# A deformable convolution sampled tile row by tile row in a loop, with part of the hat functions on GpSimd

## What is computed

```python
off1 = conv2d(x, w_off1, b_off1, stride=1, pad=1)          # 18 offsets per pixel: (dy, dx) for 9 taps
out = relu(bn_inf(deform_conv(x, off1, w_dc1, 1, 2, 2), g1, beta1, m1, v1))
off2 = conv2d(out, w_off2, b_off2, stride=1, pad=1)
out = relu(bn_inf(deform_conv(out, off2, w_dc2, 1, 2, 2), g2, beta2, m2, v2) + x)
# deform_conv: for each pixel and tap, the image is read at (y + 2*ky - 2 + dy, x + 2*kx - 2 + dx),
# bilinearly between four pixels, zero outside; then a 64 x 64 product per tap, summed over the taps
```

## Time and profile before

| | |
|---|---|
| median of 3 runs | 894.47 us (892.66 to 895.07) |
| the profiled execution | 889.64 us, span 887.6 us, mean granted TensorE clock 0.86 |
| first sampler, 40 to 255 us | 214.5 us |
| second sampler, 286 to 503 us | 216.9 us |
| attention, experts and the end, from 503 us | 384 us |
| TensorE busy, matmuls | 728.3 us, 18,746 |
| VectorE, ScalarE, GpSimd busy | 484.3, 417.0, 161.4 us |

### The profile page before, as it was taken

One profiled execution on the slowest core, in us unless ns is written; L12 is line 12 of the kernel. 1 busy time (PEld: TensorE's weight loads), 2 busy tenths in 40 slices (PEclk: granted clock), 3 DMA queues, 4 the chain that ended last, 5 costly groups with the idle time before them and its releaser, 6 DMA issues.

```text
span 887.6 us, 40461 instructions
## 1 busy us (share of the span) xinstructions
PE 728.3 (82%) x18746; PEld 567.3 (64%) x18746; DVE 484.3 (55%) x840; ACT 417.0 (47%) x830; POOL 161.4 (18%) x190
## 2 busy tenths in 40 slices
PE   6787877788767887778788656999999999999546
PEld 2355555566633455555566545999999999998433
DVE  0565554455604645446455564666666666666654
ACT  1665455554315554546544143445445445545442
POOL 7000000000030000000000153343443443341300
PEclk8889878866769798887976578999999999999669
DMA  5400000000004000000000170000000000000002
GB/s 171 82 4 5 4 4 5 5 4 4 5 6 81 4 5 4 4 4 4 5 4 4 29 193 1 1 2 1 0 0 0 0 0 0 0 0 0 0 1 96
DMA packets 7835, 16.58 MB, mean 19 GB/s; under 512 B 1982, under 2 KB 5950, under 8 KB 7286
## 3 DMA queue, kind: packets, MB, share of 16 engines
q1 hardware_dynamic: 7678, 14.21, 6.3%
HBM read 10.34 MB, written 3.87 MB: 16 GB/s over the span
## 4 chain that ended last, share of the span: by engine, by line
PE 76%; issue 10%; DVE 6%; ACT 5%; POOL 1%; DMA 1%; SPq 0%; DVEq 0%
PE banks L227 20%; PE banks L145 14%; PE banks L696 7%; PE banks L680 7%; PE banks L726 6%; PE banks L458 4%; PE banks L737 4%; PE banks L716 3%; PE banks L691 2%; PE banks L180 2%; PE banks L166 2%; PE banks L707 2%; ACT hx L273 1%; DVE norm_stats L629 1%; ACT hy L278 1%
## 5 line engine op out<-in xcount | busy, mean ns | idle before, releaser
L227 PE MATMUL banks<-s,y 32*64 32x96 f32 (+9 forms) x10752 | 191.1, 268 | 66.0 <-issue 65.9
L318 DVE TENSOR_TENSOR s<-hy,hx 128x384 f32<-128x384 f32 (+3 forms) x336 | 144.4, 476 | 183.4 <-PE banks L227 181.8
L227 PEld LDWEIGHTS banks<-s,y 32*64 32x64 f32 x10752 | 160.2, 154 | 109.9 <-issue 100.2
L145 PE MATMUL banks<-w_dc,tiled 64*32 64x192 f32 x3584 | 130.2, 412 | 20.3 <-issue 13.7
L268 ACT COPY y<-banks 128x384 f32<-128x384 f32 x192 | 81.8, 484 | 114.0 <-PE banks L145 114.0
L145 PEld LDWEIGHTS banks<-w_dc,tiled 64*32 64x32 f32 x3584 | 74.3, 131 | 53.8 <-issue 26.6
L794 ACT COPY hy<-banks 128x512 f32<-128x512 f32 x64 | 37.6, 588 | 116.7 <-PE banks L726 116.7
L278 ACT ACTIVATE hy<-banks 128x512 f32<-128x512 f32 (+2 forms) x144 | 72.9, 583 | 38.4 <-PE banks L180 38.3
L898 POOL TENSOR_TENSOR y<-y,stats 128x1024 f32<-128x1024 f32 x33 | 62.8, 1902 | 142.2 <-DVE stats L839 142.2
L273 ACT ACTIVATE hx<-banks 128x384 f32<-128x384 f32 x144 | 61.4, 505 | 31.8 <-PE banks L166 23.9
L680 PE MATMUL banks<-src,s 128*128 (+1 forms) x560 | 75.0, 279 | 1.1 <-ACT src L617 1.1
(11 more groups left out here) (137 smaller groups left out, 876.9 us busy)
## 6 DMA issues: line engine op xcount, KB each, us to landing
src<-in_x_dram SPq DMA_DIRECT2D x4, 578.0 KB, 5.5
y<-in_w_dram SPq DMA_DIRECT2D x1, 2080.0 KB
off<-in_w_dram SPq DMA_DIRECT2D x2, 1024.0 KB
out_dram<-tokens SPq DMA_DIRECT2D x4, 512.0 KB, 2.6
offsets_dram<-tokens SPq DMA_DIRECT2D x32, 54.0 KB
off<-offsets_dram SPq DMA_DIRECT2D x16, 108.0 KB
w_dc<-in_w_dc_dram SPq DMA_DIRECT2D x2, 288.0 KB, 6.0
y<-in_w_attn_dram SPq DMA_DIRECT2D x1, 512.0 KB, 4.9
```

The source lines that it names most:

```text
L145: last = nc.tensor.matmul(m.ps[32 * j:32 * j + 32, FIRST_BANK + (count + g) % RING, (col % 2) * 192:(col % 2) * 192 + 192], m.tiled[rows, ...
L227: last = nc.tensor.matmul(out[:, r0:r0 + strip.n, first:first + width], m.y[32 * j:32 * j + 32, g, (s // 3) % 2 * Y_SLOTS + strip.slot, co ...
L318: nc.vector.tensor_tensor(dst, hy, hx[:, :, r0:r0 + strip.n, :], ALU.mult).then_inc(cv.s_ready, 1)
```

## The change

The sampler's order becomes tile row, then tap: 72 steps per convolution, and a step's window is not cut at the half. TensorE runs the eight tile rows as a hardware loop; the other engines stay unrolled.

- The output of one tile row covers 12 rows. ScalarE copies four of them per tile row (eight in the first) from PSUM into `tokens`, VectorE adds the eight that overlap, ScalarE or VectorE finish four rows of the image, and TensorE clears 4 banks again. `prime`, `copied` and `added` order this.
- Columns: only the four new rows of a window are computed (`hx_near` keeps the other four from the tile row before, two slots of nine taps); new constant matrices `near_sel` (1 MB, a DMA more) and more rows of `places` make them with 4 matmuls for all four tiles. `off` is cleared by VectorE first, and SyncE waits for that before the loads of convolution 1.
- One item (x, y or weighted) now fills two banks at once and is taken by one ScalarE instruction; there are two such pairs. `s` and `hy` have three slots.
- GpSimd makes the hats in x (`sampler_pool`, 78 per convolution), copies one tile row at a time into `stage`, and doesn't tile the whole image any more.
- TensorE waits for both halves of the offsets before the sampler.
- `all_*`, the way for large offsets, is kept and not run here.

```diff
+AHEAD = 2
+STEP_WEIGHTED = {0: (2, 1, 0), 4: (0, 0, 1), 5: (0, 1, 1), 6: (1, 0, 1), 7: (1, 1, 1), 8: (2, 0, 1)}
+def slot_banks(m, k):
+    return m.ps[:, FIRST_BANK + 2 * (k % 2):FIRST_BANK + 2 * (k % 2) + 2, :]
...
+    with pe.Fori(0, TR) as i:
+        k = BEFORE_LOOP
+        for t in range(TAPS):
+            later, tap = divmod(t + AHEAD, TAPS)
+            pe.wait_ge(cv.emptied, i * PER_ROW + (k - 1))
+            columns_near(nc, m, cv, k, tap, new_rows(cv, tap) + TILE_ROWS * later, TILE_ROWS, i)
+            k += 1
+            pe.wait_ge(cv.emptied, i * PER_ROW + (k - 1))
+            rows_near(nc, m, cv, k, tap, first_row(cv, tap) + TILE_ROWS * later, i)
+            k += 1
+            if t == 0:
+                pe.wait_ge(cv.copied, i + COPIED_FROM)
+                pe.wait_ge(cv.added, i + (ADDED_FROM - 1))
+                pe.wait_ge(cv.cleared, 1)
+                for bank in range(PAIRS):
+                    nc.tensor.matmul(m.ps[:, bank, 0:OUT_ROWS * W], m.zeros[:, 0:P], m.zeros[:, 0:OUT_ROWS * W],
+                                     start=True, stop=True, skip_group_check=True)
+            if t in STEP_WEIGHTED:
+
+                pe.wait_ge(cv.emptied, i * PER_ROW + (k - 1))
...
+            pe.wait_ge(cv.s_ready, i * (2 * TAPS) + (2 * t + 2))
+            for col in range(TC):
+                first, width, skip = near_columns(cv, col, kx)
+                for j in range(4):
+                    for g in range(2):
...
+            last.then_inc(cv.sampled, 1)
+            if t in STEP_WEIGHTED:
+                weighted_near(nc, m, cv, k, *STEP_WEIGHTED[t][0:2])
+                k += 1
...
+                if t == TAPS - 1 and kind == "w" and tile_row < TR - 1:
+                    act.wait_ge(cv.sampled, TAPS * (tile_row + 1))
+                    first, n = (TILE_ROWS, 2 * TILE_ROWS) if tile_row == 0 else (2 * TILE_ROWS, TILE_ROWS)
+                    at = TILE_ROWS * (tile_row - 1) + first
+                    nc.scalar.copy(sum_rows(m, at, n), out_rows(m, first, n)).then_inc(cv.copied, 1)
+                item_act(nc, act, m, cv, k)
...
+    for n in range(TR * TAPS):
+        if n + 1 < TR * TAPS:
+            hats(n + 1)
+        if n % TAPS == 0 and n // TAPS >= 2:
+            below = n // TAPS - 1
+            dve.wait_ge(cv.sampled, n)
+            dve.wait_ge(cv.copied, COPIED_FROM + below + 1)
+            first = TILE_ROWS * (below - 1)
+            nc.vector.tensor_tensor(sum_rows(m, first, 2 * TILE_ROWS), sum_rows(m, first, 2 * TILE_ROWS),
+                                    out_rows(m, 0, 2 * TILE_ROWS), ALU.add).then_inc(cv.added, 1)
+            cv.rows_dve(dve, below - 1)
+        weights(n)
...
+def sampler_pool(nc, pool, m, cv):
+    old = 2 * cv.reach
+    for tap, tile_row in X_HATS:
+        pool.wait_ge(cv.emptied, EMPTIED_AT["x", tap, tile_row])
+        x = x_block(m, cv, tap, tile_row) if tile_row >= 0 else x_block(m, cv, tap, -1, TILE_ROWS - old, old)
+        nc.gpsimd.tensor_scalar(x, x, 1.0, 1.0, ALU.min, ALU.subtract).then_inc(cv.x_hats, 1)
+        if tap == 3 and tile_row >= 0:
+            pool.wait_ge(cv.filled, EMPTIED_AT["w", 2, 1, tile_row])
+            stage_pool(nc, m, cv, min(tile_row + 1, TR - 1))
```

More of the change, by code:

```diff
@@ L55, in near_strips @@
[L55 to L71, removed]
@@ L74, in near_columns @@
[L74 to L125, removed]
@@ new lines, in step_items @@
+def step_items(tile_row, tap):
+    items = coords(TAPS * tile_row + tap + AHEAD)
+    if tap in STEP_WEIGHTED:
+        ky, part, later = STEP_WEIGHTED[tap]
+        items.append(("w", ky, part, tile_row + later))
+    return items
+BEFORE_LOOP = len(FIRST_WEIGHTED) + len(FIRST_COORDS)
+PER_ROW = sum(len(step_items(0, tap)) for tap in range(TAPS))
+ITEMS = FIRST_WEIGHTED + FIRST_COORDS + [
+    item for tile_row in range(TR) for tap in range(TAPS) for item in step_items(tile_row, tap)]
+EMPTIED_AT = {item: k + 1 for k, item in enumerate(ITEMS)}
@@ new lines, in columns_all @@
+def columns_all(nc, pe, m, cv, count, h, tap, col):
+    pe.wait_ge(cv.all_emptied, count - RING + 2)
+    for g in range(2):
+        rows = group_rows(g, 1)
+        nc.tensor.matmul(m.ps[:, FIRST_BANK + (count + g) % RING, :],
+                         m.sel[rows, (TILE_COLS * col - 2 * (tap % 3) + 4) // 2, :],
+                         m.off[rows, tap, HALF_ROWS * W * h:HALF_ROWS * W * (h + 1)],
+                         start=True, stop=True, skip_group_check=True).then_inc(cv.all_filled, 1)
@@ new lines, in rows_all @@
+def rows_all(nc, pe, m, cv, count, h, tap, tile_row):
+    pe.wait_ge(cv.all_emptied, count - RING + 2)
+    for g in range(2):
+        rows = group_rows(g, 0)
+        nc.tensor.matmul(m.ps[:, FIRST_BANK + (count + g) % RING, :],
+                         m.sel[rows, (TILE_ROWS * tile_row - 2 * (tap // 3) + 4) // 2, :],
+                         m.off[rows, tap, HALF_ROWS * W * h:HALF_ROWS * W * (h + 1)],
+                         start=True, stop=True, skip_group_check=True).then_inc(cv.all_filled, 1)
@@ L334 @@
-ALL_SLOTS = 2
-class Row:
-    def __init__(self, tile_row, h):
-        self.tile_row, self.first, self.n, self.at = tile_row, HALF_ROWS * h, HALF_ROWS, 0
 def all_pe(nc, pe, m, cv):
-    count, n = FIRST_ITEMS, 0
+    count, n = 0, 0
     pe.wait_ge(cv.tiled, TILED)
-    pe.wait_ge(cv.moved[1], MOVES)
+    pe.wait_ge(cv.emptied, len(FIRST_WEIGHTED))
+    for half in range(HALVES):
+        pe.wait_ge(cv.moved[half], MOVES)
     for h in range(HALVES):
```

577 lines of the change are left out of this document (349 added, 228 removed).

## The result

The changed kernel takes 981.06 us (median of 4 runs, 977.49 to 985.23) where the kernel before took 894.77 (4 runs beside it): ratio 1.095, interval 1.089 to 1.102. The forecast was 933, slower by 4.3%. The direction was right; the loss is twice as large.

What follows compares the result with a forecast made beforehand. TensorE was taken as the bound, fed with code in the samplers. Looped, a serial chain would set rows of 28.0 us: first sampler +14.5, second +21, end +2, so +38 us and 933; range 878 to 998.

Steps and rivals of the forecast that it cites:

- If the body stays in place as the attention body does: TensorE's sampler loops: about 1,730 instructions stay held, so the code feed of 3.74 us per page falls away; called likelier.
- R1: Sampler loop body does not stay and code is fetched again: 992 us, or 952 with every page fetched; chance 0.25.
- The chain of 3.11 us per weighted step: Taps 5 to 8: samples, weighted fill, weighted eviction, column eviction run serially, 3.11 us a step at the upper clock level.
- The whole row: One sampler tile row: 25.9 us at the upper clock level, 31.8 at the lower, 28.0 at clock 0.80.
- The ten items ahead of the first row, 4.2 us: Start of each sampler: ten coordinate items at ScalarE's pitch of 0.38 to 0.43 take 4.2 us.
- GpSimd's hat, 0.6 us within 0.5 to 0.8: GpSimd's hat in x, 384 wide with two operations: 0.6 us each, nothing on the path.
- R3: VectorE and GpSimd hinder each other at taps 0, 2, 4: 1.8 us more a row, 962 us; chance 0.10.
- The second convolution's four small operations, 7 us: Second sampler: four small VectorE operations per row before the next products, 1.2 us in six rows, 7 us.
- The entry, 1 and 2.8 us: Before the samplers: waiting for both halves of the offsets costs 1 us in the first convolution, 2.8 in the second.
- The end, 2 us: After the second sampler: four adds more and attention weights asked for later, 2 us.
- R2: Chain does not bind and the busiest engine sets the row: 755 us, or 875 with half the chain; chance 0.20.
- 16 r + 21: Both samplers at r us a row, set equal to 431.4: the change is faster below 25.6 us a row.

Runs made afterwards that it cites:

- e1: The changed kernel with 32 small matmuls (64 instructions) added in the first convolution's never-run branch, moving only the second loop: 942.82 us, ratio 1.050.
- e2: The changed kernel with 96 small matmuls (192 instructions) in the first convolution's never-run branch: 969.15 us, ratio 1.081.
- e3: The changed kernel with 80 small matmuls (160 instructions) run once at the start, moving both loops: 1020.02 us, ratio 1.139.
- e4: The changed kernel with VectorE instead of GpSimd making the hats in x, loops placed as in the change: 972.98 us, ratio 1.085.
- e5: Loops placed as in e1; against it, the wait for the weighted item's banks moves from ahead of the samples to behind them: 939.52 us, ratio 1.042.
- e6: As e5, and the weighted item is issued between column and row item, ahead of the samples: 912.69 us, ratio 1.015.
- e11: As e7, but at tap 8 alone the weighted item stays behind the samples, as in the change: 870.63 us, ratio 0.965.
- e12: Same order as e11, with the hats in x on GpSimd as in the change: 887.83 us, ratio 0.985.
- e7: As e6, and VectorE makes the hats in x as well: 890.59 us, ratio 0.989.
- e9: As e7, with ScalarE's copy of the output rows at tap 8 moved behind the step's three items: 885.31 us, ratio 0.983.
- e10: Same order as e9, with the hats in x on GpSimd as in the change: 901.2 us, ratio 1.001.

## Why the prediction was off, by its own steps

**"If the body stays in place as the attention body does ... I take that as the likelier case."** This step failed. The question was posed for both loops at once and answered by the length of the body alone. It stayed in the first convolution and not in the second, although both are the same length, and where each one begins decides (e1, e2, e3). Of the 49.9 us by which the span missed the forecast (+87.9 against +38), the second sampler holds 40.5 (+58.6 against 18.1). e1 is the kernel that the prediction described, with both bodies in place: 1.050 where 1.043 was forecast. That closeness is partly luck, as the terms below show. R1 had the mechanism, the way back to code that is no longer held, and a price of 3.7 a row; measured it is 34.2 - 29.5 = 4.7 a turn in the second loop of the change, and 7.3 and 3.5 in the first and second loop of e3. R1 too spoke of both loops or none.

Why the place decides is argued, not shown; rows and experiments agree with one reading. In 1,716 instructions there are 6.7 blocks; they lie across seven if the loop begins within the first 77 places of a block (1,716 is 6 x 256 + 180), and across eight otherwise. If eight blocks are held and one of them is always the block ahead, seven stay and eight do not, and a loop across eight fetches nine a turn, as measured. The Trainium skill, "Runtime: NRT & Kernel Launch", section "Instruction fetch mechanics", gives TensorE a FIFO of 2,048 instructions in blocks of 256, that is eight. The trace agrees with that size only by this reading, and the last way back of e3, with its 0.22 us and no fetch, doesn't fit it. The prediction set 1,730 against 2,048 and wrote that it "would just fit"; by this reading it left out the block that is fetched ahead and the two ends of the body. The listing's places 224 and 225 would then be near a block's start on the chip, so by this reading listing and chip differ by a constant that no run here measured.

**The chain of 3.11 us per weighted step** was right in kind and close in size: 3.28. Its terms, with what was predicted in brackets: samples 0.99 with their drain (0.85), weighted copy 0.80 (0.80), the next one starting 0.70 after it (0.68), column eviction 0.50 (0.51). The whole row is 27.15 at a granted clock of 1.00, where 25.9 was computed for the upper level: 0.7 more in the four chain steps, 0.4 at tap 1 (3.22 against 2.8), 0.6 at tap 3 (2.05 against 1.45; e4 has 1.66 there, so 0.4 of it is GpSimd's hat), and 0.3 less at tap 0, whose copy is 512 wide and not 1024 (0.58 us against 1.01). 28.0 was used, because the clock was assumed to stay at 0.80 and was 0.97. **The ten items ahead of the first row, 4.2 us:** from the first coordinate matmul to the first samples it is 8.6 in both samplers. That the first sampler took 229.2 against 228 is luck: the start was 4.4 too short and the eight rows together 3.4 too long. e5 showed that the chain has a twin through the row fill; e6 and e11 showed that the order of issue holds these steps, worth 0.6 to 0.7 us a step.

**GpSimd's hat, 0.6 us within 0.5 to 0.8:** mis-sized, 1.59. The nearest rows were a copy and a two-input product of 512; an instruction with a scalar operation and 384 elements is dearer than both. It cost little all the same, since it has a step of 2.0 to 3.3 us to hide in, though not the nothing that was predicted: 0.7 us a turn (e4). In e12 against e11 it costs 17 us in all, of which 0.6 a turn, 8 to 9 us, lie in turns 2 to 8 of the two loops and 5 in their first rows (23.8 against 21.6 us from the first samples on, and 26.0 against 23.0). So something like R3 happened, at less than half its price of 1.8 a row; how much of it is the hat's length and how much the two engines' hindering each other wasn't separated.

**R3's mechanism** shows in the rows of one tap: the product of 0.86 us at 165.49 runs from its start to its end while GpSimd's hat of 1.64 runs from 165.40 on. In the whole trace 84 products start and end within one hat: 0.69 us in the mean and 0.86 at most, against 0.55 for the 75 beside no GpSimd work; and a hat takes 1.49 with VectorE idle (11 of them) and 1.61 with a product beside it (124). Both are slowed and neither is stopped. The Trainium skill, "SBUF — State Buffer", section "Who interferes with whom", calls the shared pair "an exclusive lock"; the trace agrees that the two engines hinder each other, and not that the one that came first keeps the other out to its end, which would have held this product until 167.04 (it ended at 166.35). GpSimd's spans in a profile are rough, so how far each is slowed is an estimate.

**The second convolution's four small operations, 7 us:** in e1 its turns average 29.5 us against 27.2 in the first loop, 2.2 us a turn, 16 in seven turns. The two of its turns that ran at a granted clock of 1.00 throughout take 28.6 and 28.3 against 27.15, 1.2 to 1.4 a turn, so about 9 of the 16 are these operations, near the 7 that were computed, and the rest goes with the clock, which was 0.83 to 0.94 in the other five.

**The entry, 1 and 2.8 us:** 4.3 and 4.9. TensorE stands until the second half of the offsets is there; the first coordinate matmuls of the two samplers, in TensorE's timeline:

```profile
44.50 0.80 PE L130 MATMUL banks<-off,near_sel 128*128 128x128 bf16 x8 [9.68 <-DMA off<-offsets_dram]
...
310.06 0.80 PE L130 MATMUL banks<-off,near_sel 128*128 128x128 bf16 x8 [8.60 <-DMA off<-offsets_dram]
```

Whether a wait for the first half alone would give this back was not tried; by the code it would not do as the kernel stands: the window of a later tap begins above its own first row, and so reads the end of the tap before, which comes with the second half. **The end, 2 us:** 5.4, and 4.4 of them lie behind the attention loop, in code that both kernels share. Busy time of that stretch, before and after, columns as in the earlier trace rows:

```profile
818.28:887.60 69.32, 38.05 (x492) 25.69 (x492) 38.06 (x57) 23.90 (x35) 9.49 (x6) 0.79 0.08 31
901.76:975.50 73.74, 42.76 (x492) 28.55 (x492) 38.07 (x57) 24.22 (x35) 9.49 (x6) 0.74 0.07 29
```

The same stretch takes 69 us at a granted clock of 0.79 in e1, e2 and e11 and 74 at 0.74 in e3 to e7, e9, e10 and e12, so two single profiles can differ there by 4.7 us whatever the sampler does; that holds for 4.7 of the 19.6 us between the spans of e12 and e11 too.

**R2** didn't happen: the chain binds. Rows under its 25.6 us came only once the order of issue had shortened the chain: e11 has rows of 24 us and is faster than before. By the prediction's own 16 r + 21 a row of 24 is 26 us under the kernel before, 2.9%; e11 is 3.5% under it. The times given for R2 don't follow from that sum: a row of 22 us makes 836 and not 875, one of 17.4 makes 762 and not 755.

## What to carry to other kernels

A loop saves the code feed only if its body stays in place, and for this body of 1,716 instructions the place where it begins decided that. Count instruction packets per turn on the engine's instruction queue; a few dozen instructions that never run, ahead of the loop, were worth 4% of this kernel. Once the feed is gone, the order of issue comes next. List every item that waits for the same eviction before you move one: taking away one of two equal branches gave nothing here, and taking away both gave 30 us. And don't hand an elementwise step to GpSimd because VectorE is half idle: VectorE did it in 358 ns where GpSimd took 1,593. Last, compare turns at the same granted clock before you compare totals.

## What the runs showed of the hardware that was not expected

- 64 dead instructions move a kernel by 38 us; the backward branch takes 0.21 to 0.26 us in loops that fetch nothing and 3.6 to 5.1 where the blocks are fetched anew.
- GpSimd's tensor-scalar over 128x384 fp32 in place: 1.24 us with one operation, 1.59 to 1.62 with two (1.17 and 1.49 with VectorE idle). VectorE's: 0.36.
- TensorE's granted clock went from 0.80 in the unrolled samplers, where it stood between blocks of code, to 0.97 in turns 2 to 8 of the first loop and 0.89 in those of the second. The stops of 4 us at the way back don't account for the second's lower clock: e1 has none and stands at 0.91 there, and e2 has them and stands at 0.92.
